# Routed experts: a third buffer for the weighed outputs, single inner buffers, and a gather issued ahead of the scatter

## The chip, the cores and the metric

The kernel runs on one core of a Trainium2 chip. The metric is the device time of one execution in microseconds (us); lower is better.

## The reference, cut to what matters

The model is x + 0.5·FFN, then x + attention, then x + 0.5·FFN again, on 4 x 1024 tokens of width 512 in float32. The two FFN halves have the same weights and hold the change. Each sends a token to 6 of 32 experts, with at most 192 tokens (slots) per expert:

```python
g = einsum('ech,eih->eci', xb, w_gate)      # xb: the tokens of expert e, gathered
u = einsum('ech,eih->eci', xb, w_up)
inter = silu(g) * u
yb = einsum('eci,ehi->ech', inter, w_down)
y = yb[eid, pos] * w_slot[:, None]          # weighed by the router
routed = y.reshape(-1, K, Hd).sum(axis=1)   # six weighed rows are added per token
```

A shared expert is added for every token; in the kernel a stage before this one computes it.

## The kernel before, in words

The program is: front, routed experts, attention, front, routed experts. `front` (n=0 and n=1) normalises the tokens, computes the router and the shared expert, stores the normalised rows in the HBM table `htab`, and makes `slots`, the row numbers of each expert's two halves of 96 tokens. The change lies in `routed_experts` alone, which runs once per FFN half, over e = 0 to 31. For one expert:

- **gather(e)** (L901, GpSimd, software queue q0): two indirect DMAs fetch 96 rows of 544 floats each from `htab` into `e_xg`. There are GATHERED = 5 such pairs of buffers, and five gathers are issued before the loop.
- **turn(e)**: TensorE transposes the rows (8 transposes, L1052), ScalarE and VectorE split them into a high and a low part (L930, L995).
- **Weights**: SyncE loads three thirds of 512 KB (L876, hardware queue q1) into one of three `e_raw` buffers; ScalarE makes the high part (L925), VectorE the low one (L989). Before the load of expert e+3, SyncE waits until scatter e-3 has landed (`added`, only for e of 3 and more) and until VectorE has split the expert e, third by third.
- **gate_up(e)**: 32 matmuls (L1063, L1064). ScalarE and VectorE add the parts, take the SiLU (L942), the product (L1009, `inter`) and split it into `in_hi` (L947) and `in_lo` (L1014).
- **down(e)**: 12 matmuls into two PSUM banks (L89 to L91).
- **weigh(e)** (L954, ScalarE): two activations write the weighed rows to `y`, which has two pairs of buffers (e % 2). So weigh(e) waits until scatter e-2 has landed. It also reads its scale from `e_xg`, so gather(e+5), which refills that buffer, may be issued only after it.
- **scatter(e)** (L909, GpSimd, q0): two indirect DMAs add 96 rows each to the result in HBM. It waits for weigh(e) and for the landing of scatter(e-1), since two experts may add to one token.

Each engine runs its own list of these steps in a written-out order. In iteration e TensorE does turn(e+1), gate_up(e), down(e-1). ScalarE does turn(e+1), two thirds of split(e+1), SiLU(e), weigh(e-1), split_inner(e), the last third of split(e+1). VectorE follows the same order. GpSimd does scatter(e), then gather(e+5) if there is one. In the first FFN half ten pieces of the attention weights are loaded and split as well. SyncE, ScalarE, VectorE and TensorE meet GpSimd only through semaphores. The stage ends when scatter(31) has landed, and the next stage begins behind it. After gather(31), which follows scatter(26), GpSimd has only scatters to issue.

Of the kernel before, what the change touches and what calls it, by code (L numbers as in the profile page):

```python
# [7 lines left out]
F32 = mybir.dt.float32  # L8
F32R = mybir.dt.float32r
# [3 lines left out]
ALU = mybir.AluOpType  # L13
ACT = mybir.ActivationFunctionType
AX = mybir.AxisListType

P = 128
B, SEQ, D = 4, 1024, 512
# [6 lines left out]
HALF = CAP // 2  # L25
# [59 lines left out]
def split_products(pe, out, hi_lo_weights, hi_lo_moving, first, last):  # L85

    wh, wl = hi_lo_weights
    mh, ml = hi_lo_moving
    pe.matmul(out, wh, mh, start=first, stop=False)  # L89
    pe.matmul(out, wh, ml, start=False, stop=False)  # L90
    return pe.matmul(out, wl, mh, start=False, stop=last)  # L91
# [731 lines left out]
def routed_experts(nc, a, k, n, htab, acc, slots, raw, xs, w_loaded, y_stored):  # L823

    with ExitStack() as ctx:
        sb = lambda name, shape, dt: ctx.enter_context(nc.sbuf_tensor(f"{name}{n}", shape, dt))
        pb = lambda name: ctx.enter_context(nc.psum_tensor(f"{name}{n}", [P, 512], F32))
        sem = lambda name: own_semaphore(nc, k, f"{name}{n}")
        TC = 2 * CAP
# [4 lines left out]
        xt = [sb(f"e_xt{u}_", [P, KB, 2, CAP], F32R) for u in range(2)]  # L834
        gate_low, up_low = sb("e_gate_low", [P, FB, CAP], F32), sb("e_up_low", [P, FB, CAP], F32)
        gate_sum, up_sum = sb("e_gate_sum", [P, FB, CAP], F32), sb("e_up_sum", [P, FB, CAP], F32)
        silu = [sb(f"e_silu{u}_", [P, TC], F32) for u in range(2)]
        inter = [sb(f"e_inter{u}_", [P, TC], F32) for u in range(2)]
        in_hi = [sb(f"e_in_hi{u}_", [P, TC], F32R) for u in range(2)]
        in_lo = [sb(f"e_in_lo{u}_", [P, TC], F32R) for u in range(2)]  # L840
        y = [[sb(f"e_y{u}{q}_", [HALF, D], F32) for q in range(2)] for u in range(2)]
        ps_t = [pb(f"e_ps_t{i}_") for i in range(2)]
        ps_gate = ctx.enter_context(nc.psum_tensor(f"e_ps_gate{n}", [P, FB * 512], F32))
        ps_up = ctx.enter_context(nc.psum_tensor(f"e_ps_up{n}", [P, FB * 512], F32))
        ps_down = [pb(f"e_ps_down{q}_") for q in range(2)]
        gathered = [sem(f"e_gathered{r}_") for r in range(GATHERED)]
        added = sem("e_added")
# [6 lines left out]
        ihi_ready, ilo_ready = sem("e_ihi_ready"), sem("e_ilo_ready")  # L854
        d_ready, y_ready = sem("e_d_ready"), sem("e_y_ready")
# [15 lines left out]
        with nc.Block(no_gpsimd_drain=True) as block:  # L871
# [24 lines left out]
            @block.gpsimd  # L896
            def _(pool):
                def gather(e):
                    for q in range(2):
                        row = bass.IndirectOffsetOnAxis(ap=slots[:, 2 * e + q:2 * e + q + 1], axis=0)  # L900
                        pool.indirect_dma_start(xg[e % GATHERED][q][:, :], None, htab, row).then_inc(gathered[e % GATHERED], 16)  # L901

                def scatter(e):
                    pool.wait_ge(y_ready, 2 * e + 2)
                    if e:
                        pool.wait_ge(added, 32 * e)
                    for q in range(2):
                        row = bass.IndirectOffsetOnAxis(ap=slots[:, 2 * e + q:2 * e + q + 1], axis=0)
                        pool.indirect_dma_start(acc, row, y[e % 2][q][:, :], None, compute_op=ALU.add).then_inc(added, 16)  # L909

                for e in range(GATHERED):
                    gather(e)
                for u in range(XS):
                    pool.wait_ge(y_stored[u], 16 * ((NT - 1 - u) // XS + 1))
                for e in range(E):
                    scatter(e)
                    if e + GATHERED < E:
                        gather(e + GATHERED)
                pool.wait_ge(added, 32 * E)

            @block.scalar
            def _(act):
                def split(e, c):
                    act.wait_ge(w_loaded[e % 3][c], 16 * (e // 3) + 16)
                    act.activation(third(w_hi[e % 2], c), third(raw[e % 3], c), ACT.Copy).then_inc(hi_ready, 1)  # L925

                def turn(e):
                    for c in range(2):
                        act.wait_ge(t_ready, 2 * e + c + 1)
                        act.activation(part(xt[e % 2], c, 0), turned(c), ACT.Copy).then_inc(t_hi, 1)  # L930

                def unload_gate(e):
                    act.wait_ge(gate_ready, e + 1)
                    act.activation(gate_low[:, :, :], low(ps_gate), ACT.Copy).then_inc(gate_low_ready, 1)

                def unload_up(e):
                    act.wait_ge(up_ready, e + 1)
                    act.activation(up_low[:, :, :], low(ps_up), ACT.Copy).then_inc(up_low_ready, 1)

                def gate(e):  # L940
                    act.wait_ge(gate_sum_ready, e + 1)
                    act.activation(silu[e % 2][:, :], gate_sum[:, :, :].rearrange("p b s -> p (b s)"),  # L942
                                   ACT.Silu).then_inc(silu_ready, 1)

                def split_inner(e):
                    act.wait_ge(mul_ready, e + 1)
                    act.activation(in_hi[e % 2][:, :], inter[e % 2][:, :], ACT.Copy).then_inc(ihi_ready, 1)  # L947

                def weigh(e):
                    if e >= 2:  # L950
                        act.wait_ge(added, 32 * (e - 1))
                    for q in range(2):
                        act.wait_ge(d_ready, 2 * e + q + 1)
                        act.activation(y[e % 2][q][:, :], ps_down[q][0:HALF, :], ACT.Copy,  # L954
                                       scale=xg[e % GATHERED][q][:, D + e:D + e + 1]).then_inc(y_ready, 1)

                def split_chunk(c):
                    hi, lo, from_ = attention_chunks[c]
                    act.wait_ge(att_loaded[c % XS], 16 * (c // XS) + 16)
                    act.activation(hi, xs[c % XS][:, :], ACT.Copy).then_inc(att_hi, 1)  # L960

                split(0, 0)
                split(0, 1)
                turn(0)
                split(0, 2)
                for e in range(E):
                    ahead = e + 1 < E
                    if ahead:
                        turn(e + 1)
                        split(e + 1, 0)  # L970
                    unload_gate(e)
                    if ahead:
                        split(e + 1, 1)
                    gate(e)
                    unload_up(e)
                    if e:
                        weigh(e - 1)
                    split_inner(e)
                    if ahead:
                        split(e + 1, 2)  # L980
                    if 0 <= e - 1 < len(attention_chunks):
                        split_chunk(e - 1)
                weigh(E - 1)

            @block.vector
            def _(dve):
# [19 lines left out]

                def gate(e):
                    dve.wait_ge(silu_ready, e + 1)
                    dve.tensor_tensor(inter[e % 2][:, :], silu[e % 2][:, :], up_sum[:, :, :].rearrange("p b s -> p (b s)"),  # L1009
                                      ALU.mult).then_inc(mul_ready, 1)  # L1010

                def split_inner(e):
                    dve.wait_ge(ihi_ready, e + 1)
                    dve.tensor_tensor(in_lo[e % 2][:, :], inter[e % 2][:, :], in_hi[e % 2][:, :].bitcast(F32),  # L1014
                                      ALU.subtract).then_inc(ilo_ready, 1)

                def split_chunk(c):
# [25 lines left out]
            def _(pe):  # L1043
# [34 lines left out]
                def down(e):  # L1078
                    w = [t[e % 2][:, WGU:].rearrange("p (k c) -> p k c", k=FB) for t in (w_hi, w_lo)]
                    pe.wait_ge(lo_ready, 3 * e + 3)  # L1080
                    pe.wait_ge(ilo_ready, e + 1)
                    for q in range(2):
                        if e:
                            pe.wait_ge(y_ready, 2 * e + q - 1)
                        for b in range(FB):
                            s = slice(b * CAP + q * HALF, b * CAP + (q + 1) * HALF)
                            got = split_products(pe, ps_down[q][0:HALF, :], (in_hi[e % 2][:, s], in_lo[e % 2][:, s]),
                                                 (w[0][:, b, :], w[1][:, b, :]), b == 0, b == FB - 1)
                        got.then_inc(d_ready, 1)

                turn(0)
                for e in range(E):
                    if e + 1 < E:
                        turn(e + 1)
                    gate_up(e)
                    if e:
                        down(e - 1)
                down(E - 1)


# [609 lines left out]
```

## Time and profile before

| what | value |
|---|---|
| median of 3 runs | 1670.54 us (1665.2 to 1672.09) |
| the profiled execution | 1662.59 us, span 1660.8 us |
| PE busy | 1476.0 us (89%) |
| VectorE, ScalarE, GpSimd busy | 1103.8, 1028.3, 754.6 us |
| 64 scatter DMAs of the first half, of the second | 96.4 us, 95.7 us on GpSimd |
| first and last scatter issue, first half | 247.58 and 527.30 us |
| first and last scatter issue, second half | 1381.37 and 1656.13 us |

All positions are in us from the start of the span. A row of the timeline gives start, duration, engine, line, operation and, in brackets, the idle time before it and what ended that. "DMA out<-e_y,slots" is the scatter in the second FFN half, "DMA x_after_ffn<-e_y,slots" that in the first.

### The profile page before, as it was taken

Reading aid. Unit: us, or ns where it says so; the run is one execution under the profiler, and the core shown is the slowest. Engines: PE = TensorE matmul, PEld = TensorE weight load, DVE = VectorE, ACT = ScalarE, POOL = GpSimd, SP = SyncE. Lnnn points to the kernel's source line nnn. Section 1 sums busy time; section 2 is a strip of 40 time slices with the busy share of each in tenths; the row PEclk is TensorE's granted clock in tenths of the full one; section 3 lists DMA queues with packets and bytes.
Section 4 is the critical chain, followed back from the end, with each engine's and each line's share of the span. In section 5 each row is a group of like instructions: output and inputs, shape, how many; then the busy total and the mean of one; then the engine's idle time right before and its main releaser. Section 6 shows DMA issues by size and latency. Waiting matters only on the chain. (4 is left out here: it accounts for less than half of the span.)

```text
span 1660.8 us, 23985 instructions
## 1 busy us (share of the span) xinstructions
PE 1476.0 (89%) x8434; PEld 1226.3 (74%) x8436; DVE 1103.8 (66%) x2094; ACT 1028.3 (62%) x2046; POOL 754.6 (45%) x655
## 2 busy tenths in 40 slices
PE   5999969989894889999999999895999869998896
PEld 4877768877773678887887887774887758877775
DVE  5659848867672466766766765664649858776774
ACT  5861448777773476666666666654762528776774
POOL 0123225655554666565556655420113224665554
PEclk9999979999997799999999999997999979999998
DMA  7736388989895101111111111006654467998895
GB/s 275 246 126 207 99 260 249 266 257 265 258 264 87 52 26 46 39 58 52 39 39 64 39 39 39 30 35 232 204 178 153 144 205 231 259 270 250 263 257 104
DMA packets 113207, 257.61 MB, mean 155 GB/s; under 512 B 21216, under 2 KB 22176, under 8 KB 112832
## 3 DMA queue, kind: packets, MB, share of 16 engines
q1 hardware_dynamic: 90560, 204.16, 37.3%
q0 software_dynamic: 22528, 51.92, 13.8%
q8 instruction: 68, 1.11, 0.3%
q14 instruction: 51, 0.42, 0.1%
HBM read 187.27 MB, written 68.76 MB: 154 GB/s over the span
## 5 line engine op out<-in xcount | busy, mean ns | idle before, releaser
L989 DVE TENSOR_TENSOR e_w_lo<-e_raw,e_w_hi 128x1024 fp32r<-128x1024 f32 x192 | 233.9, 1219 | 31.2 <-ACT e_w_hi L925 29.6
L925 ACT ACTIVATE e_w_hi<-e_raw 128x1024 fp32r<-128x1024 f32 x192 | 202.3, 1054 | 20.8 <-PEq L273 20.8
L1490 POOL TENSOR_SCALAR t_prob<-t_prob,t_inv 128x128 f32<-128x128 f32 (+7 forms) x128 | 111.5, 871 | 221.3 <-DVE t_inv L1395 221.3
L901 POOL DMA_INDIRECT e_xg<-htab,slots x128 | 145.7, 1138 | 58.0 <-issue 38.4
L1063 PE MATMUL e_ps_gate<-e_xt,e_w_hi 128*128 128x384 f32 x512 | 159.3, 375 | 0.0
L909 POOL DMA_INDIRECT x_after_ffn<-e_y,slots x64 | 96.4, 1506 | 121.8 <-ACT e_y L954 83.9
L1063 PE MATMUL e_ps_up<-e_xt,e_w_hi 128*128 128x384 f32 x512 | 151.0, 360 | 0.0
L909 POOL DMA_INDIRECT out<-e_y,slots x64 | 95.7, 1495 | 120.9 <-ACT e_y L954 83.6
L357 POOL TENSOR_SCALAR d_inter<-d_inter 128x512 f32<-128x512 f32 x32 | 26.2, 818 | 266.9 <-DVE d_inter L521 266.8
L1290 ACT ACTIVATE t_prob<-a_wide,t_neg_max,a_q_scale 128x128 f32<-128x128 f32 (+7 forms) x128 | 106.5, 832 | 53.8 <-DVE t_neg_max L1389 53.5
L954 ACT ACTIVATE e_y<-e_ps_down,e_xg 96x512 f32<-96x512 f32 x128 | 83.1, 679 | 90.5 <-DMA out<-e_y,slots 34.2
L1064 PE MATMUL e_ps_gate<-e_xt,e_w_lo 128*128 128x192 f32 x512 | 130.5, 255 | 0.0
L1064 PE MATMUL e_ps_up<-e_xt,e_w_lo 128*128 128x192 f32 x512 | 128.4, 251 | 0.0
L1297 ACT ACTIVATE t_pt<-a_bank 128x512 fp32r<-128x512 f32 x144 | 84.0, 596 | 68.4 <-PE a_bank L1566 68.1
L1400 DVE TENSOR_TENSOR t_pt<-a_bank,t_pt 128x512 fp32r<-128x512 f32 x144 | 96.2, 684 | 41.6 <-ACT t_pt L1297 41.0
L1052 PE MATMUL e_ps_t<-ident,e_xg 96*128 96x96 f32 x512 | 58.1, 259 | 69.2 <-DMA e_xg<-htab,slots 69.2
L1052 PEld LDWEIGHTS e_ps_t<-ident,e_xg 96*128 96x128 f32 x512 | 48.0, 146 | 93.5 <-DMA e_xg<-htab,slots 91.4
L1014 DVE TENSOR_TENSOR e_in_lo<-e_inter,e_in_hi 128x384 fp32r<-128x384 f32 x64 | 35.8, 559 | 111.8 <-ACT e_in_hi L947 108.8
L89 PE MATMUL e_ps_down<-e_w_hi,e_in_hi 128*96 128x512 f32 x256 | 101.4, 396 | 3.6 <-issue 3.6
L91 PE MATMUL e_ps_down<-e_w_hi,e_in_lo 128*96 128x512 f32 x256 | 101.8, 398 | 0.0
L90 PE MATMUL e_ps_down<-e_w_lo,e_in_hi 128*96 128x512 f32 x256 | 100.9, 394 | 0.0
L1064 PEld LDWEIGHTS e_ps_gate<-e_xt,e_w_lo 128*128 128x128 f32 x512 | 100.8, 197 | 0.1
(218 smaller groups left out, 4613.5 us busy)
## 6 DMA issues: line engine op xcount, KB each, us to landing
e_raw<-in_w_experts SPq DMA_DIRECT2D x192, 512.0 KB
htab<-d_h SPq DMA_DIRECT2D x16, 1024.0 KB, 5.2
d_x<-in_x SPq DMA_DIRECT2D x16, 512.0 KB, 6.9
d_xs<-in_x SPq DMA_DIRECT2D x32, 256.0 KB, 3.5
x_after_ffn<-d_xs SPq DMA_DIRECT2D x32, 256.0 KB, 3.2
q_x<-x_after_ffn SPq DMA_DIRECT2D x32, 256.0 KB, 3.0
t_res<-x_after_ffn SPq DMA_DIRECT2D x32, 256.0 KB, 2.6
x_after_attention<-t_res SPq DMA_DIRECT2D x32, 256.0 KB, 2.0
```

Of the source, the lines that this page charges most:

```text
L89: pe.matmul(out, wh, mh, start=first, stop=False)
L90: pe.matmul(out, wh, ml, start=False, stop=False)
L91: return pe.matmul(out, wl, mh, start=False, stop=last)
L901: pool.indirect_dma_start(xg[e % GATHERED][q][:, :], None, htab, row).then_inc(gathered[e % GATHERED], 16)
L909: pool.indirect_dma_start(acc, row, y[e % 2][q][:, :], None, compute_op=ALU.add).then_inc(added, 16)
L925: act.activation(third(w_hi[e % 2], c), third(raw[e % 3], c), ACT.Copy).then_inc(hi_ready, 1)
L989: dve.tensor_tensor(third(w_lo[e % 2], c), third(raw[e % 3], c), third(w_hi[e % 2], c).bitcast(F32), ALU.subtract).then_inc(lo_ready, 1)
L1052: got = pe.transpose(ps_t[c][:, at:at + HALF], xg[e % GATHERED][q][:, (2 * c + b) * P:(2 * c + b + 1) * P], k.ident[0:HALF, 0:HALF])
L1063: pe.matmul(out, w[0][:, c, cols], xt[e % 2][:, c, :, :], start=c == 0, stop=False)
L1064: got = pe.matmul(out[:, 0:CAP], w[1][:, c, cols], xt[e % 2][:, c, 0, :], start=False, stop=c == KB - 1)
L1290: act.activation(prob[:, u, 0:width(i)], ps_s[i % 2][:, 0:width(i)], ACT.Exp, scale=q_scale[:, i // H % QSLOTS, i % H:i % H + 1], bias=neg ...
L1490: pool.tensor_scalar(prob[:, u, 0:width(i)], prob[:, u, 0:width(i)], inv[:, u:u + 1], 1.0, ALU.mult, ALU.mult).then_inc(p_ready, 1)
```

## The change

`silu`, `inter`, `in_hi` and `in_lo` get one buffer each in place of two. `y` gets a third pair of buffers, so weigh(e) waits for the landing of scatter e-3. GpSimd's loop waits for weigh(e) first, then issues gather(e+5), and then waits for the landing of scatter(e-1) and issues scatter(e).

```diff
-        silu = [sb(f"e_silu{u}_", [P, TC], F32) for u in range(2)]
-        inter = [sb(f"e_inter{u}_", [P, TC], F32) for u in range(2)]
-        in_hi = [sb(f"e_in_hi{u}_", [P, TC], F32R) for u in range(2)]
-        in_lo = [sb(f"e_in_lo{u}_", [P, TC], F32R) for u in range(2)]
-        y = [[sb(f"e_y{u}{q}_", [HALF, D], F32) for q in range(2)] for u in range(2)]
+        silu = sb("e_silu", [P, TC], F32)
+        inter = sb("e_inter", [P, TC], F32)
+        in_hi = sb("e_in_hi", [P, TC], F32R)
+        in_lo = sb("e_in_lo", [P, TC], F32R)
+        y = [[sb(f"e_y{r}{q}_", [HALF, D], F32) for q in range(2)] for r in range(3)]
...
                 def scatter(e):
-                    pool.wait_ge(y_ready, 2 * e + 2)
                     if e:
                         pool.wait_ge(added, 32 * e)
...
-                        pool.indirect_dma_start(acc, row, y[e % 2][q][:, :], None, compute_op=ALU.add).then_inc(added, 16)
+                        pool.indirect_dma_start(acc, row, y[e % 3][q][:, :], None, compute_op=ALU.add).then_inc(added, 16)
...
                 for e in range(E):
-                    scatter(e)
+                    pool.wait_ge(y_ready, 2 * e + 2)
                     if e + GATHERED < E:
                         gather(e + GATHERED)
+                    scatter(e)
...
                 def weigh(e):
-                    if e >= 2:
-                        act.wait_ge(added, 32 * (e - 1))
+                    if e >= 3:
+                        act.wait_ge(added, 32 * (e - 2))
```

The remaining lines replace `[e % 2]` of the four inner buffers by the single one, and `y[e % 2]` by `y[e % 3]`.

## Rows read from the trace of the kernel before

**Rows 1.** The page: its head, and its chain that ended last, by line.
```profile
span 1660.8 us, 23985 instructions
...
DMA out<-e_y,slots 11%; POOL out L909 3%; ACT e_y L954 1%; DMA e_xg<-htab,slots 1%; POOL e_xg L901 0%; PE e_ps_gate L1063 0%; PE e_ps_up L1063 0%; PE e_ps_t L1052 0%; DVE e_w_lo L989 0%; PE e_ps_gate L1064 0%; PE e_ps_up L1064 0%; ACT e_w_hi L925 0%; PE e_ps_down L91 0%; PE e_ps_down L89 0%; DVE e_xt L995 0%
```

**Rows 2.** Windows: stretch, length, busy PE, PEld, DVE, ACT, POOL, PEclk, DMA, GB/s.
```profile
1390.50:1444.40 53.90, 53.10 (x340) 46.49 (x338) 44.05 (x62) 43.28 (x73) 34.69 (x24) 1.00 0.91 266
1444.40:1527.30 82.90, 73.96 (x468) 63.53 (x468) 58.34 (x81) 59.86 (x100) 46.44 (x37) 1.00 0.88 260
```

**Rows 3.** The chain that ended last, in order of time, 1501 to 1518.
```profile
1501.26 6.73 DMA out<-e_y,slots
...
1508.01 0.69 ACT e_y L954
...
1508.79 1.47 POOL out L909
...
1510.56 6.14 DMA out<-e_y,slots
...
1517.50 1.46 POOL out L909
```

**Rows 4.** Waits, 1450 to 1600: total, times, longest (us).
```profile
POOL out L909 <- ACT e_y L954: 52.8, 17, 4.0
...
ACT e_y L954 <- DMA out<-e_y,slots: 27.6, 16, 2.7
PEld e_ps_t L1052 <- DMA e_xg<-htab,slots: 22.8, 16, 2.1
```

**Rows 5.** Waits of the queue on SyncE, 1376 to 1445, and 1445 to 1620.
```profile
SPq L876 <- DMA out<-e_y,slots: 45.8, 7, 8.4
...
SPq L876 <- DMA out<-e_y,slots: 147.0, 19, 8.6
```

**Rows 6.** DMA queues (packets, MB, share), 1509.8 to 1512.8, and 1514.2 to 1517.2.
```profile
q1 hardware_dynamic: 315, 1.16, 97.3%
...
q0 software_dynamic: 315, 0.75, 101.2%
```

**Rows 7.** Timeline of GpSimd, start of the second stage, then of the first.
```profile
1381.37 1.83 POOL L909 DMA_INDIRECT out<-e_y,slots  x1 [18.88 <-ACT e_y L954]
1383.51 1.44 POOL L909 DMA_INDIRECT out<-e_y,slots  x1 [0.30 <-issue]
1385.25 1.07 POOL L901 DMA_INDIRECT e_xg<-htab,slots  x1 [0.30 <-issue]
1386.62 1.29 POOL L901 DMA_INDIRECT e_xg<-htab,slots  x1 [0.30 <-issue]
1389.88 2.44 POOL L909 DMA_INDIRECT out<-e_y,slots  x1 [1.96 <-DMA out<-e_y,slots]
...
257.75 1.46 POOL L909 DMA_INDIRECT x_after_ffn<-e_y,slots  x1 [2.96 <-DMA x_after_ffn<-e_y,slots]
```

**Rows 8.** Timeline of ScalarE: weigh(0), (1), (2) second half, (8); weigh(1) of the first stage.
```profile
1379.24 1.25 ACT L954 ACTIVATE e_y<-e_ps_down,e_xg 96x512 f32<-96x512 f32 x2
1386.79 1.36 ACT L954 ACTIVATE e_y<-e_ps_down,e_xg 96x512 f32<-96x512 f32 x2
1395.46 0.68 ACT L954 ACTIVATE e_y<-e_ps_down,e_xg 96x512 f32<-96x512 f32 x1 [0.45 <-PE e_ps_down L91]
1443.64 1.29 ACT L954 ACTIVATE e_y<-e_ps_down,e_xg 96x512 f32<-96x512 f32 x2 [1.44 <-DMA out<-e_y,slots]
...
253.66 1.25 ACT L954 ACTIVATE e_y<-e_ps_down,e_xg 96x512 f32<-96x512 f32 x2
```

**Rows 9.** The chain that ended last, at its end: the scatter with no other traffic.
```profile
1642.78 4.25 DMA out<-e_y,slots
1647.79 1.41 POOL out L909
```

**Rows 10.** Windows, behind the first stage (columns as in Rows 2).
```profile
528.00:536.00 8.00, 0.00 (x0) 0.00 (x0) 1.25 (x2) 1.28 (x1) 0.72 (x1) 0.50 0.62 136
```

More of the change, by code:

```diff
@@ L941, in gate @@
                     act.wait_ge(gate_sum_ready, e + 1)
-                    act.activation(silu[e % 2][:, :], gate_sum[:, :, :].rearrange("p b s -> p (b s)"),
+                    act.activation(silu[:, :], gate_sum[:, :, :].rearrange("p b s -> p (b s)"),
                                    ACT.Silu).then_inc(silu_ready, 1)
@@ L946, in split_inner @@
                     act.wait_ge(mul_ready, e + 1)
-                    act.activation(in_hi[e % 2][:, :], inter[e % 2][:, :], ACT.Copy).then_inc(ihi_ready, 1)
+                    act.activation(in_hi[:, :], inter[:, :], ACT.Copy).then_inc(ihi_ready, 1)
                 def weigh(e):
-                    if e >= 2:
-                        act.wait_ge(added, 32 * (e - 1))
+                    if e >= 3:
+                        act.wait_ge(added, 32 * (e - 2))
                     for q in range(2):
                         act.wait_ge(d_ready, 2 * e + q + 1)
-                        act.activation(y[e % 2][q][:, :], ps_down[q][0:HALF, :], ACT.Copy,
+                        act.activation(y[e % 3][q][:, :], ps_down[q][0:HALF, :], ACT.Copy,
                                        scale=xg[e % GATHERED][q][:, D + e:D + e + 1]).then_inc(y_ready, 1)
@@ L1008, in gate @@
                     dve.wait_ge(silu_ready, e + 1)
-                    dve.tensor_tensor(inter[e % 2][:, :], silu[e % 2][:, :], up_sum[:, :, :].rearrange("p b s -> p (b s)"),
+                    dve.tensor_tensor(inter[:, :], silu[:, :], up_sum[:, :, :].rearrange("p b s -> p (b s)"),
                                       ALU.mult).then_inc(mul_ready, 1)
@@ L1013, in split_inner @@
                     dve.wait_ge(ihi_ready, e + 1)
-                    dve.tensor_tensor(in_lo[e % 2][:, :], inter[e % 2][:, :], in_hi[e % 2][:, :].bitcast(F32),
+                    dve.tensor_tensor(in_lo[:, :], inter[:, :], in_hi[:, :].bitcast(F32),
                                       ALU.subtract).then_inc(ilo_ready, 1)
@@ L1086, in down @@
                             s = slice(b * CAP + q * HALF, b * CAP + (q + 1) * HALF)
-                            got = split_products(pe, ps_down[q][0:HALF, :], (in_hi[e % 2][:, s], in_lo[e % 2][:, s]),
+                            got = split_products(pe, ps_down[q][0:HALF, :], (in_hi[:, s], in_lo[:, s]),
                                                  (w[0][:, b, :], w[1][:, b, :]), b == 0, b == FB - 1)
```

## The prediction

> **What bounds the kernel now.** I read the chain that ended last on the page first [rows 1]. What it names for the last stage is one thing: the scatter's DMA, 11% of the span, with its issue on GpSimd, 3%. In the table of stretches [rows 2] the reader is to see two regimes in one stage. From 1390.5 to 1444.4 TensorE is busy 53.10 of 53.90 us; an expert is 52 matmuls and transposes (8 + 32 + 12), so 340 of them are 6.5 experts at 8.2 us each. From 1444.4 on it is busy 89%, and 468 are 9.0 experts in 82.9 us, 9.2 us each. The clock is full in both. So TensorE could run at 8.2 and is held to 9.2.
>
> The chain in order of time says by what [rows 3]. The second half of scatter(13) is issued at 1501.26 and lands 6.73 us later, at 1507.99; weigh(15) starts at 1508.01; scatter(14) is issued at 1508.79. The profile puts ScalarE between them, but weigh(15) fills the buffer for scatter(15), and scatter(14) waits for landing(13) alone: it starts 0.80 us after it, as scatter(31) does where ScalarE has long been done (landing at 1642.78 + 4.25 = 1647.03 for scatter(30), issue at 1647.79, 0.76 later [rows 9]). The loop is therefore: first issue 1.47, gap 0.30, second issue to landing 6.14, wake 0.80 = 8.71 us, and 9.1 on average. It is strictly serial over 32 experts and no buffer is in it. The waits of ScalarE for the scatter (16 times, 27.6 us) and of TensorE for the gather (16 times, 22.8 us) [rows 4] are the other engines held to that loop: one through the `y` buffer, one because the gather is issued behind the scatter.
>
> What fills 6 to 7 us of landing, when the last scatters need 4.25 [rows 9]? SyncE's loads wait for the same landing, 7 times to 1445 and in all 19 experts of 1445 to 1620, for 147.0 us [rows 5], so 1.5 MB of weights start at each landing. The queues show it [rows 6]: in 1509.8 to 1512.8 the hardware queue holds 97.3% of the engines and q0 moves nothing, though scatter(14) and a gather have been issued; in 1514.2 to 1517.2 q0 has them. Landing, weights, then scatter, is one cycle.
>
> **The change, part by part.**
>
> *Single inner buffers.* ScalarE writes `in_hi`(e) behind weigh(e-1), which has waited for down(e-1), the reader of the old one; VectorE's writes come behind its own reads and ScalarE's. The written order covers them: 0. If it did not, a copy would be late on an engine that gains 0.9 us per expert on the scatters.
>
> *Third `y` buffer.* Removed: weigh(e)'s wait for landing(e-2); in its place is landing(e-3). ScalarE and TensorE may run one expert further ahead. They gain about 9.1 - 8.2 = 0.9 us per expert, so the wait that now begins at weigh(8) [rows 8] begins some ten experts later and then comes back at the same size. Next late is the gather, then the weights: load(e+3) is released by landing(e-3), so a third needed about 3 us behind a landing would just arrive. None of it reaches the scatter loop, which has its `y` ready either way. On the path: 0. If that cover were gone, ScalarE's 27.6 us / 16 = 1.7 us per expert would be the price.
>
> *Gather ahead, in the steady stretch.* Scatter(e-1)'s second issue ends about 4 us after landing(e-2). weigh(e) is done by 1.3 us after landing(e-2) even with two buffers [rows 3], earlier with three. So GpSimd finds `y_ready` set and issues gather(e+5) at once behind scatter(e-1), in the very place where gather(e+4) is now. Its order of instructions and q0's order of packets are the same, with the gather's number one higher. Both run under the landing. SyncE's loads are tied to the landings as before. Cost 0 per expert.
>
> *Gather ahead, at the start.* Here there is no cover. GpSimd is free and waits for weigh(0), done at 1380.49 [rows 8]; scatter(0) follows at 1381.37. Now gather(5) is put between: 1.07 + 0.30 + 1.29 + 0.30 = 2.96 us as they stand behind the scatter [rows 7]. Scatter(0)'s two issues move by that. Its landing moves by less or by more: second issue 1383.51, landing 1389.88 - 0.80 = 1389.08, so 5.57, of which 4.25 is needed without traffic. A weight third that shares this time would be over: at best the landing moves by 2.96 - 1.32 = 1.6; with the gather's rows ahead in q0 (a half of the 0.75 MB that took 3 us [rows 6], 1.5 us) at worst by 4.5. I take 2.5, near the issues' own time, the nearest row.
>
> Expert 1: weigh(1) is done at 1388.15, GpSimd starts gather(6) at about 1389.0 and ends it at 1391.9; landing(0) is now at 1391.6, scatter(1) could go at 1392.4. Hidden on GpSimd, but its rows are ahead in q0 just when the weights burst starts: between 0 and 1.5 us, I take 0.5. Expert 2: weigh(2) is done at 1396.14, scatter(1)'s issues end near 1396, so the gather starts a microsecond later than now: 0. From expert 3 on the lead is enough.
>
> The first FFN half: weigh(1) is done at 254.91 and scatter(1) starts at 257.75 [rows 7, 8], a wider cover; scatter(0) is followed by the same pair. Again 2.5.
>
> *The end.* gather(31) moves from behind scatter(26) to behind scatter(25). Its rows come behind the scatter's: between 0 and -1.5 us, I take 0. TensorE ends a period earlier, but it is already at the 1.2 GHz level (0.50) before attention starts [rows 10], so its clock there is unchanged: 0.
>
> Sum: 2 x 2.5 + 0.5 = 5.5, with bounds 2 x 1.6 - 2 x 1.5 = 0 and 2 x (4.5 + 1.5) = 12. I take +5. The profiled execution is 1662.59 (span 1660.8), 8 us under the median of 1670.54; on that median's scale the forecast is 1675.5, its own range 1669 to 1683. About 0.5% (8 us) is what a measurement of this kernel can tell from no change.
>
> **The rivals.**
>
> *A, slower: the gather delays the scatters beyond the start.* Place: GpSimd, between `y_ready`(e) and scatter(e). It decides where weigh(e) ends later than about 2 us before landing(e-1), since the two gather issues take 2.5 to 3. In the stages' first experts the lead is 0.9 us at expert 1 (1388.15 against 1389.08) and grows by 0.9 each. If three experts per stage pay 2.96 and 1.5 us of rows in q0: 2 x 3 x 4.46 = +27; with issues alone +18. For: it is certain for e = 0. Against: every later `y_ready` is ahead. Middle +20: 1690.5.
>
> *B, slower: VectorE at full pace lengthens the issues.* In the stretch where VectorE does not wait, a scatter issue took 2.44 us (1389.88) against 1.47 [rows 7, 3]; it lies in the serial loop. The change lengthens that stretch by some ten experts per stage: 2 x 10 x 0.97 = +19 at most, with the 5: 1695. Against: the stretch before 1444 has the same 9.1 us per scatter, since the scatter's rows wait for the weights anyway. The Trainium skill ("SBUF — State Buffer", "Who interferes with whom") says that a VectorE instruction with two SBUF inputs contends with a GpSimd one that reads SBUF; the long issue above agrees.
>
> *C, faster: landings get shorter.* Two neighbours take 6.73 and 6.14 us [rows 3], and I do not know why. If TensorE's and ScalarE's lead shifts the traffic so that all take the short one, 0.6 us for half of 50 steady experts is 15 us, and 30 if for all: with the 5 added, about 1660, down to 1645. Against: loads and scatters are both tied to the landing.
>
> *D: no change at all,* the start hidden by shorter contention: 1670.5. It lies in the forecast's own range.
>
> The Trainium skill ("DMA: Bandwidth & Descriptors", "Queues, rings and completion order") says that an engine takes turns between queues packet by packet; by that the scatter would share with the weights, where here q0 moved nothing for 3 us. By the page a gather ahead in q0 would cost about twice its own 1.5 us, by the row 1.5.
>
> **How the numbers follow.** Forecast with D 0.67 (nine tenths of it within 0.5%, the rest slower), A 0.10, B 0.05, C 0.15, other 0.03, shared. Faster: C's larger part and a little of the rest, 0.14. Slower: A, B and the forecast's upper tail, 0.20. Same: 0.66. The range 1660 to 1689 holds the forecast, D, half of A and half of C.
>
> **What the profile would show.** Right: GpSimd issues two gathers, then scatter(0), some 3 us later after weigh(0) than now; from expert 3 on the sequence is scatter, scatter, gather, gather; the mean step between scatters stays at 9.1; ScalarE's wait for the scatter starts near expert 18; 3 to 5 us more between weigh(0) and the last landing of each stage. Wrong: a step between scatters that differs from 9.1 by over 0.2 us (6 us per stage), gathers between a landing and a scatter behind expert 3, or weights loads no longer released by the landing.

## The result and the profile after

The changed kernel has a median of 1673.22 us (1668.40 to 1675.36, 12 runs) against 1666.97 us of the kernel before (1663.64 to 1672.09, 12 runs): ratio 1.0033, 95% interval 1.0018 to 1.0048, so 5.5 us slower. (Where a cost in us is given for a kernel, it is this ratio less 1, times the median of the kernel before; the two medians themselves are 6.25 us apart.) Forecast were +5 and "within 0.5%". The absolute forecast of 1675.5 stood on a median of three runs, 1670.54, which twelve runs put at 1666.97. The profiled execution took 1668.4 us, its span is 1666.5.

The page of the changed kernel, its head and the chain by line (as [rows 1]):

```profile
span 1666.5 us, 23931 instructions
...
DMA out<-e_y,slots 12%; POOL out L908 3%; POOL e_xg L901 1%; DMA e_xg<-htab,slots 0%; ACT e_y L954 0%; PE e_ps_gate L1063 0%; DVE e_w_lo L989 0%; PE e_ps_up L1063 0%; PE e_ps_t L1052 0%; PE e_ps_gate L1064 0%; ACT e_w_hi L925 0%; DVE e_xt L995 0%; ACT e_up_low L938 0%; PE e_ps_up L1064 0%; DVE e_inter L1009 0%
```

The scatter is still what the last stage is made of. GpSimd's timeline at the start of the second stage, as [rows 7]:

```profile
1382.02 0.92 POOL L901 DMA_INDIRECT e_xg<-htab,slots  x1 [18.98 <-ACT e_y L954]
1383.25 1.72 POOL L901 DMA_INDIRECT e_xg<-htab,slots  x1 [0.31 <-issue]
1385.27 2.36 POOL L908 DMA_INDIRECT out<-e_y,slots  x1 [0.30 <-issue]
1387.93 1.45 POOL L908 DMA_INDIRECT out<-e_y,slots  x1 [0.30 <-issue]
1389.68 1.25 POOL L901 DMA_INDIRECT e_xg<-htab,slots  x1 [0.30 <-issue]
1391.24 1.31 POOL L901 DMA_INDIRECT e_xg<-htab,slots  x1 [0.30 <-issue]
1392.85 2.27 POOL L908 DMA_INDIRECT out<-e_y,slots  x1 [0.30 <-issue]
...
1403.27 1.46 POOL L908 DMA_INDIRECT out<-e_y,slots  x1 [3.03 <-DMA out<-e_y,slots]
```

gather(5) stands ahead of scatter(0), which starts 5.29 us behind the start of weigh(0) (1379.98) and not 2.13. gather(6) already stands directly behind scatter(0)'s second issue, in the place that gather(5) had; scatter(1) follows it at once, and from scatter(2) on GpSimd waits for the landing again. In the first stage the same rows are:

```profile
248.96 1.49 POOL L908 DMA_INDIRECT x_after_ffn<-e_y,slots  x1 [0.30 <-issue]
250.76 1.45 POOL L908 DMA_INDIRECT x_after_ffn<-e_y,slots  x1 [0.30 <-issue]
...
255.87 1.49 POOL L908 DMA_INDIRECT x_after_ffn<-e_y,slots  x1 [0.30 <-DMA x_after_ffn<-e_y,slots]
```

Here scatter(1) follows scatter(0) after 6.91 us, where it took 10.17 before (247.58 to 257.75): the delayed scatter(0) landed at most 4.3 us behind its second issue, as the last scatters do that meet no weights. From weigh(0) to scatter(2) the first stage lost 0.9 us and the second 3.3 (against the second profile of before, told below, 1.0 and 2.4).

The waits of 1450 to 1600 (as [rows 4]) and, below the dots, SyncE's from 1445 to 1620 (as [rows 5]): total, times, longest.

```profile
POOL out L908 <- DMA out<-e_y,slots: 40.2, 17, 3.7
...
ACT e_y L954 <- DMA out<-e_y,slots: 22.3, 15, 2.4
PEld e_ps_t L1052 <- DMA e_xg<-htab,slots: 19.7, 15, 1.8
...
ACT e_w_hi L925 <- DMA e_raw<-in_w_experts: 5.7, 15, 0.6
...
SPq L876 <- DMA out<-e_y,slots: 147.1, 19, 9.3
```

As forecast, the stalls came back at nearly their size (ScalarE's 22.3 us against 27.6, TensorE's 19.7 against 22.8), the loads are released by the landings as before (147.1 against 147.0 us), and a new small wait for the weights, 5.7 us in 15 times, stands where a third of weights "would just arrive". The windows (columns as in [rows 2]):

```profile
1391.20:1449.00 57.80, 57.80 (x379) 51.81 (x378) 47.45 (x67) 47.94 (x81) 35.76 (x26) 1.00 0.89 256
1449.00:1532.00 83.00, 76.37 (x483) 65.61 (x481) 62.01 (x86) 61.54 (x103) 52.84 (x37) 1.00 0.89 260
```

TensorE's lead goes on longer, and ScalarE first waits for a landing at weigh(11):

```profile
1467.31 1.48 ACT L954 ACTIVATE e_y<-e_ps_down,e_xg 96x512 f32<-96x512 f32 x2 [0.42 <-DMA out<-e_y,slots]
```

The mean step between scatters 3 and 26 is 9.22 us in the first stage and 9.18 in the second, against 9.18 and 9.15 before. That difference is inside what one kernel shows from execution to execution, as the run named before_again tells below. So one trace shows a start that costs something, and cannot show whether the steady stretch costs a tenth of a microsecond per expert. The medians had to decide that.

### The profile page after: what moved, and what is told of

Its sections match the earlier page's. It is cut to its first block and busy times, and to the rows that moved or that the text cites. A ratio compares the mean times of both kernels' runs of the same rounds, so it can differ in the third digit from the quotient of the medians.

```text
span 1666.5 us, 23931 instructions
## 1 busy us (share of the span) xinstructions
PE 1472.3 (88%) x8434; PEld 1224.6 (73%) x8436; DVE 1104.7 (66%) x2094; ACT 1028.9 (62%) x2046; POOL 771.3 (46%) x655
## 5 line engine op out<-in xcount | busy, mean ns | idle before, releaser
L989 DVE TENSOR_TENSOR e_w_lo<-e_raw,e_w_hi 128x1024 fp32r<-128x1024 f32 x192 | 234.2, 1221 | 34.0 <-ACT e_w_hi L925 29.8
L901 POOL DMA_INDIRECT e_xg<-htab,slots x128 | 158.7, 1240 | 96.8 <-ACT e_y L954 40.3
L908 POOL DMA_INDIRECT out<-e_y,slots x64 | 100.1, 1565 | 95.0 <-DMA out<-e_y,slots 71.0
L908 POOL DMA_INDIRECT x_after_ffn<-e_y,slots x64 | 97.4, 1522 | 98.2 <-DMA x_after_ffn<-e_y,slots 74.0
```

The source lines that it names most:

```text
L908: pool.indirect_dma_start(acc, row, y[e % 3][q][:, :], None, compute_op=ALU.add).then_inc(added, 16)
L989: dve.tensor_tensor(third(w_lo[e % 2], c), third(raw[e % 3], c), third(w_hi[e % 2], c).bitcast(F32), ALU.subtract).then_inc(lo_ready, 1)
```

## The experiments

**Theory T** (the prediction's): the loop of scatters is the bound; only the gather ahead of scatter(0) costs. **Rival R**: the other engines' greater lead lengthens the landings.

**The two parts alone.** third_buffer_only restores the old order on top of the changed kernel:

```diff
                     pool.wait_ge(y_ready, 2 * e + 2)
+                    scatter(e)
                     if e + GATHERED < E:
                         gather(e + GATHERED)
-                    scatter(e)
```

> Third y buffer and single inner buffers, with the gather behind the scatter as before. Theory T (the loop of scatters is the bound, and only the gather put ahead of scatter(0) costs): no change against the kernel before, ratio 0.999 to 1.001; scatter(0) again 0.9 us behind the end of weigh(0), the step from scatter(26) to scatter(27) again about 9.0. Rival R (the greater lead of the other engines shifts the traffic and lengthens the landings): slower, 1.002 to 1.004, with the loss spread over the experts.

Measured: 1671.42 us, 1.0028 (1.0018 to 1.0038). T is wrong here and R has the size: the third buffer alone, which I had put at 0, costs 4.7 us. R's premise, the greater lead, is looked at below. gather_ahead_only puts the new order into the kernel before, with two `y` buffers:

> The new order on GpSimd with two y buffers and the old inner buffers. T: the whole loss of the change, ratio 1.002 to 1.005, in the first expert of each stage (scatter(0) 3 to 4 us behind weigh(0)). R: no change, since the lead is that of the kernel before.

Measured: 1671.52 us, 1.0028 (1.0017 to 1.0039). T has the size of this part, and scatter(0) starts 5.3 us behind the start of weigh(0) as it says. But from weigh(0) to scatter(2) the two stages lose 3.3 us together (2.5 against the second profile of before), so T's "in the first expert" leaves 1.4 to 2.2 us without a place. The parts cost 4.7 us each and together 5.5, so they do not add up: either one costs 0.28% in the kernel before and about 0.05% on top of the other (1.0033 against 1.0028, inside the intervals).

first_gather_behind takes the changed kernel and moves gather(5) alone back:

```diff
-                    if e + GATHERED < E:
+                    if e and e + GATHERED < E:
                         gather(e + GATHERED)
                     scatter(e)
+                    if e == 0:
+                        gather(GATHERED)
```

> The changed kernel, but gather(5) alone goes back behind scatter(0); gather(6) and the later ones stay ahead. T: most of the loss is gone, ratio 1.000 to 1.002 (what is left is gather(6) ahead of scatter(1)). If the loss comes from the later experts or from the end of the stage, where scatter(27) started 10.1 us behind scatter(26) in the changed kernel: still 1.002 to 1.004.

Measured: 1672.73 us, 1.0022 (1.0010 to 1.0034). This is T's miss (1.000 to 1.002) and inside the other forecast. 0.0011 or 1.8 us less than the changed kernel, within both intervals. The start may hold a part of the loss, not most of it. What is left has the size of the third buffer's own cost, but that it is that cost is not shown.

**Is it the freed wait, or the layout?** third_buffer_no_lead keeps three buffers and the layout of third_buffer_only but the old wait:

```diff
-                    if e >= 3:
-                        act.wait_ge(added, 32 * (e - 2))
+                    if e >= 2:
+                        act.wait_ge(added, 32 * (e - 1))
```

> As third_buffer_only (three y buffers, single inner ones, gather behind the scatter), but weigh(e) waits for landing(e-2) as in the kernel before, so that ScalarE and TensorE cannot run further ahead. third_buffer_only measured 1.0028. If the lead makes that loss (theory L): 0.999 to 1.001, mean step between scatters 3 to 26 back at 9.1 to 9.2, and the second scatter issue back at 1.44 us from 1.62. If the other places of the buffers in SBUF make it (rival P): 1.002 to 1.004, step 9.3.

Measured: 1667.95 us, 0.9999 (0.9988 to 1.0010). The intervals of third_buffer_only (1.0018 to 1.0038) and of this kernel (0.9988 to 1.0010) do not meet. It is the wait that weigh(e) no longer has, and neither the layout nor the single inner buffers. The forecast of the step, back at 9.1 to 9.2, missed: it is 9.27 and 9.30 us here and 9.30 and 9.35 in third_buffer_only, and one trace does not tell these apart.

The name is misleading in one thing: third_buffer_only has no greater lead to lose. From expert 8 to 25 weigh(e) ends on average 7.7 and 8.1 us before landing(e-1) in its two stages, against 7.8 and 7.8 in the kernel before. The gather, issued behind the scatter, still holds TensorE (23.8 us in 15 waits from 1450 to 1600, against 22.8 in 16), and through it ScalarE. Only where the gather is ahead as well, in the changed kernel, does the lead grow, to 16.1 us. Weigh(14), second half, and scatter(14) in third_buffer_only; then weigh(15) and scatter(15) in the changed kernel:

```profile
1502.47 0.68 ACT L954 ACTIVATE e_y<-e_ps_down,e_xg 96x512 f32<-96x512 f32 x1 [0.65 <-PE e_ps_down L91]
1512.40 1.47 POOL L908 DMA_INDIRECT out<-e_y,slots  x1 [1.82 <-DMA out<-e_y,slots]
```

```profile
1504.66 1.26 ACT L954 ACTIVATE e_y<-e_ps_down,e_xg 96x512 f32<-96x512 f32 x2 [1.26 <-DMA out<-e_y,slots]
1523.23 1.47 POOL L908 DMA_INDIRECT out<-e_y,slots  x1 [2.65 <-DMA out<-e_y,slots]
```

So a greater lead, R's mechanism, does not explain the 4.7 us of third_buffer_only. What the pages do show are GpSimd's issues. For each kernel: all gathers, then the scatters of the first stage. Before_again, third_buffer_no_lead, third_buffer_only, and the changed kernel; last, the gathers of gather_ahead_only:

```profile
L901 POOL DMA_INDIRECT e_xg<-htab,slots x128 | 146.4, 1144 | 58.0 <-issue 38.4
L909 POOL DMA_INDIRECT x_after_ffn<-e_y,slots x64 | 97.0, 1515 | 119.5 <-ACT e_y L954 77.7
```

```profile
L901 POOL DMA_INDIRECT e_xg<-htab,slots x128 | 149.3, 1167 | 58.0 <-issue 38.4
L908 POOL DMA_INDIRECT x_after_ffn<-e_y,slots x64 | 99.5, 1554 | 117.2 <-ACT e_y L954 62.7
```

```profile
L901 POOL DMA_INDIRECT e_xg<-htab,slots x128 | 158.0, 1234 | 58.0 <-issue 38.4
L908 POOL DMA_INDIRECT x_after_ffn<-e_y,slots x64 | 101.0, 1578 | 111.5 <-ACT e_y L954 62.8
```

```profile
L901 POOL DMA_INDIRECT e_xg<-htab,slots x128 | 158.7, 1240 | 96.8 <-ACT e_y L954 40.3
L908 POOL DMA_INDIRECT x_after_ffn<-e_y,slots x64 | 97.4, 1522 | 98.2 <-DMA x_after_ffn<-e_y,slots 74.0
```

```profile
L901 POOL DMA_INDIRECT e_xg<-htab,slots x128 | 160.8, 1256 | 95.1 <-ACT e_y L954 38.3
```

GpSimd's issues become longer: the 128 gathers go from 146 and 149 to 158 us. The scatters' second issues, experts 8 to 25, take 1.58 to 1.66 us on average in third_buffer_only and 1.56 to 1.59 in the changed kernel, against 1.44 to 1.51 in third_buffer_no_lead and the two profiles of before. That is rival B's sign. But it does not come from a lead: gather_ahead_only, with two `y` buffers, has it too (160.8 us, and 1.56 to 1.57). Nor is VectorE busier under the issues: it works in 96 to 97% of the gathers' time before and in 91% in third_buffer_only and third_buffer_no_lead alike. What has changed is that a gather beside its split of the weights takes longer (L989: 1.32 and 1.33 us in the two profiles of before, 1.37 in third_buffer_no_lead, 1.41 in third_buffer_only, 1.59 in gather_ahead_only); why is not known. So every kernel of this group that is 0.2 to 0.3% slower has longer issues, which would also fit that the two parts do not add up. Whether they are the price is the next question.

before_again, the kernel before once more:

> The kernel before once more, for a second profile: how much the mean step between scatters (9.1 in the first), the durations of the issues and the totals of the stages (308.4 and 304.1 us from the first gather to the last scatter issue) scatter between executions of one kernel. If the differences between the variants are of the kernel, the second scatter issue is again at 1.44 us and the totals stay within 2 us; if they are of the execution, they move by as much as between the variants, 5 us.

Measured: 1669.03 us. The second scatter issue takes 1.47 and 1.44 us on average (experts 8 to 25), as in the first profile (1.44 both times); as far as two executions tell, it belongs to the kernel. From the first gather to the last scatter issue the stages took 306.0 and 309.8 us against 308.4 and 304.1: up to 5.7 us apart. So totals and mean steps (9.33 against 9.14 from scatter 8 to 26 of the second stage) do not separate kernels that differ by 0.3%.

**What stands in the loop?** gather_behind_landing makes each gather wait for landing(e-1):

```diff
                     if e + GATHERED < E:
+                        if e:
+                            pool.wait_ge(added, 32 * e)
                         gather(e + GATHERED)
```

> The changed kernel, but gather(e+5) waits for landing(e-1) like the scatter, so that both its issues stand openly in the loop between landing and scatter in 26 experts of each stage. If the issue time is in the loop in full, 2.5 us x 52 = 130 us slower (ratio 1.078), with the gather's rows in q0 ahead up to 3.5 x 52 = 180 (1.11). If the weights burst behind each landing covers the issues, since the scatter's rows wait for it anyway, only the rows ahead in q0 count: 1.2 to 1.5 us x 52 = 62 to 78 us (1.037 to 1.047).

Measured: 1740.88 us, 1.0435 (1.0420 to 1.0450), 72.5 us: the covered case. Beside the changed kernel, which it differs from by this edit alone, it is 67 us or 1.3 per expert. GpSimd's timeline of this kernel:

```profile
1504.18 0.96 POOL L901 DMA_INDIRECT e_xg<-htab,slots  x1 [3.68 <-DMA out<-e_y,slots]
1505.45 1.69 POOL L901 DMA_INDIRECT e_xg<-htab,slots  x1 [0.30 <-issue]
1507.44 1.51 POOL L908 DMA_INDIRECT out<-e_y,slots  x1 [0.30 <-issue]
1509.26 1.43 POOL L908 DMA_INDIRECT out<-e_y,slots  x1 [0.30 <-issue]
1514.28 1.55 POOL L901 DMA_INDIRECT e_xg<-htab,slots  x1 [3.58 <-DMA out<-e_y,slots]
```

The gathers add 3.26 us ahead of the scatter, but from its second issue to the landing (0.8 before 1514.28) it is 4.2 us now and not 6.1 to 6.7 [rows 3]. The burst of weights has passed by the time the scatter's rows come. Some 2 us of this delay behind the landing are covered.

issue_delay puts two memsets, each with a drain, at the same place in third_buffer_no_lead:

```diff
                         pool.wait_ge(added, 32 * e)
+                        pool.memset(pad[:, :], 0.0)
+                        pool.drain()
+                        pool.memset(pad[:, :], 0.0)
+                        pool.drain()
```

> third_buffer_no_lead (0.9999 of the kernel before) with two memsets of 128x480 on GpSimd between the landing of scatter(e-1) and the issue of scatter(e), some 1.0 to 1.4 us with their drains in 31 experts of each stage. If the issue time stands in the loop in full: 62 to 87 us slower, ratio 1.037 to 1.052; then the longer issues of the variants with a lead (2 to 5 us per stage) explain their 0.3 per cent. If the weights burst behind the landing covers it: at most the last 5 experts of each stage, which have no load, pay, 10 to 14 us, ratio 1.006 to 1.008; then longer issues are not the cause.

Measured: 1821.91 us, 1.0928 (1.0897 to 1.0960), outside both. The dose was not what I meant it to be:

```profile
1536.17 0.51 POOL L907 MEMSET e_pad<- 128x480 f32 x1
1539.85 0.50 POOL L909 MEMSET e_pad<- 128x480 f32 x1 [3.17 <-issue]
1541.18 1.47 POOL L913 DMA_INDIRECT out<-e_y,slots  x1 [0.83 <-issue]
1542.95 1.67 POOL L913 DMA_INDIRECT out<-e_y,slots  x1 [0.30 <-issue]
1544.92 0.97 POOL L902 DMA_INDIRECT e_xg<-htab,slots  x1 [0.30 <-issue]
1546.19 1.76 POOL L902 DMA_INDIRECT e_xg<-htab,slots  x1 [0.30 <-issue]
1547.95 0.52 POOL L907 MEMSET e_pad<- 128x480 f32 x1
```

The first drain, behind the gathers, holds GpSimd for 3.17 us, and GpSimd itself is the bound: it has no wait for a landing left in a step of 11.8 us. ScalarE's weigh, released at 1535.86, shows landing to issue as 5.3 us and not 0.8. As a test of a small dose it failed. It leaves rival B undecided: 4.5 us more before the issue lengthened the step from 9.3 to 11.7, so here too about 2 us were covered, which speaks against a price for issues that are 0.1 to 0.2 us longer; but no small dose was measured, and both doses lie ahead of the first issue, not in the second.

**Is it the weights that make the landing long?** small_loads:

```diff
-                    sp.dma_start(third(raw[e % 3], c), third(a["w_experts"][e, :, :], c)).then_inc(w_loaded[e % 3][c], 16)
+                    size = THIRD if e < 6 else THIRD // 4
+                    sp.dma_start(third(raw[e % 3], c)[:, 0:size], third(a["w_experts"][e, :, :], c)[:, 0:size]).then_inc(w_loaded[e % 3][c], 16)
```

> The changed kernel with the weights of expert 6 and later loaded to a quarter only (the rest of each third keeps what an earlier expert left there). If weights traffic fills the landing, it falls to the 4.2 to 4.3 us of the last scatters, the loop would take 1.77 + 4.3 + 0.8 = 6.9 us, TensorE becomes the bound and the step is 8.0 to 8.2: 0.9 to 1.1 x 22 x 2 = 40 to 48 us faster, ratio 0.971 to 0.976. If the landing is long for another reason (the accumulation in HBM, the gather behind it): step 9.0 and no change.

This kernel leaves out three quarters of the weights from expert 6 on. Measured: 1606.1 us, 0.9634 (0.9618 to 0.9649). The window from 1400 to 1500 (columns as in [rows 2]):

```profile
1400.00:1500.00 100.00, 100.00 (x649) 89.14 (x648) 81.81 (x115) 81.77 (x138) 82.27 (x51) 1.00 0.77 153
```

TensorE never stops, 52 instructions take 8.0 us, and scatters follow each other in 7.99 us. The bound has moved as forecast; it gained 61 us and not 40 to 48: the steps fell by 1.2 us, which over 23 experts of two stages is 55, and the first steps shrank too. loads_ungated keeps the bytes and removes the tie:

```diff
-                    if e >= 3:
-                        sp.wait_ge(added, 32 * (e - 2))
```

> The changed kernel without SyncE's wait for the landing of scatter e-3; the loads follow VectorE's splits alone. If the burst of weights at each landing is what makes the scatter's landing 6 to 7 us (the cycle of the prediction): the loads spread out, the step between scatters falls from 9.1 towards TensorE's 8.2, at most 0.9 x 26 x 2 = 47 us faster, ratio 0.97 to 0.99. If the DMA engines' total work is the bound, however it is spread (busy 0.90): no change or up to 1 per cent slower, step 9.1 to 9.3.

Measured: 1648.48 us, 0.9889 (0.9874 to 0.9903). The same edit without the change, before_ungated:

> The kernel before, with SyncE's loads freed from the landing of scatter e-3, nothing else. The changed kernel with that edit measured 0.9889. If the change's third buffer and order are of use once the loads no longer come in a burst at the landing: this one is slower than that, 0.992 to 0.997. If the gain is the gate's alone and the change costs its 0.3 per cent here too: 0.984 to 0.987.

Measured: 1667.35 us, 0.9998 (0.9984 to 1.0013), slower than either case: here the freed loads gain nothing, and the change is worth 1.1%. third_ungated:

> The same edit on third_buffer_only (three y buffers, gather behind the scatter). Beside before_ungated it tells what the lead does without the burst: if the lead's loss came from its meeting with the burst, this is equal to before_ungated or faster by up to 0.5 per cent; if not, slower by 0.3 per cent.

Measured: 1666.36 us, 0.9984 (0.9969 to 1.0000): beside before_ungated no clear difference, and not the 0.3% of third_buffer_only. By the forecast's own terms the third buffer's loss then came from its meeting with the burst of loads behind each landing. Its second scatter issues are long here too (1.56 and 1.61 us) and cost nothing that shows, which speaks against rival B. What is left to make use of the freed loads is the order on GpSimd, and the last kernel, ahead_ungated, has just that with two `y` buffers:

> gather_ahead_only (two y buffers, the gather ahead of the scatter) with the loads freed from the landing. Against the kernel before, the freed loads gave 0.9998 without the change, 0.9984 with the third buffer alone, 0.9889 with the whole change. If the order on GpSimd is what makes use of the freed loads: 0.987 to 0.992. If order and third buffer are needed together: 0.996 to 1.001.

Measured: 1626.7 us, 0.9750 (0.9732 to 0.9769), beyond the forecast of the first case and the fastest kernel of this study that computes the whole reference. Windows of 1400 to 1600 (columns as in [rows 2]) of before, before_ungated, loads_ungated and ahead_ungated:

```profile
1400.00:1600.00 200.00, 183.27 (x1161) 157.83 (x1160) 146.01 (x203) 147.95 (x247) 115.75 (x89) 1.00 0.90 263
```

```profile
1400.00:1600.00 200.00, 184.12 (x1145) 162.33 (x1144) 145.74 (x201) 147.06 (x245) 123.45 (x88) 0.97 0.97 264
```

```profile
1400.00:1600.00 200.00, 191.39 (x1209) 170.42 (x1208) 153.22 (x212) 153.37 (x256) 134.68 (x94) 0.97 1.01 280
```

```profile
1400.00:1600.00 200.00, 195.91 (x1263) 173.94 (x1263) 157.19 (x220) 158.95 (x267) 135.41 (x94) 1.00 1.01 275
```

Instructions in brackets tell the pace: 1161, 1145, 1209 and 1263 in 200 us, or 9.0, 9.1, 8.6 and 8.2 us per expert. With the loads freed TensorE still waits for gathers, whether they stand behind the scatter (before_ungated) or ahead of it with three `y` buffers (loads_ungated), and the waits are few and long. The waits of the one and then of the other, 1480 to 1600:

```profile
PEld e_ps_t L1050 <- DMA e_xg<-htab,slots: 11.5, 6, 4.1
```

```profile
PEld e_ps_t L1050 <- DMA e_xg<-htab,slots: 10.3, 4, 4.8
```

In ahead_ungated that wait is absent from 1480 to 1600, and TensorE's clock is full. Against it loads_ungated has the third `y` buffer, and the single inner ones, and is 1.4% slower (0.9889 against 0.9750). Here the slower kernel does have the longer lead: weigh(e) ends 11.7 and 10.3 us before landing(e-1), against 6.6 and 6.4 (experts 8 to 25). Which of the two buffer changes costs the 1.4% was not tried.

## Why the prediction was right, and which step of it was not

- *The bound.* Right, and shown. Less weights traffic brings the step to TensorE's 8.0 us; a scatter whose issue comes behind the burst lands in 4.2 us.
- *Single inner buffers, 0.* Right where it was tried: third_buffer_no_lead has them and measures 0.9999. Together with the long lead of the changed kernel they were not tried apart.
- *Third `y` buffer, 0.* **Wrong**, taken alone: it costs 0.28%, 4.7 us, and with the old wait at weigh(e) nothing; on top of the gather ahead it adds 0.05%, which is no clear difference. The step that failed is "None of it reaches the scatter loop". I had reasoned about waits, and no wait does reach it. Nor does ScalarE run "one expert further ahead" by the third buffer alone: its lead stays at 8 us until the gather goes ahead too. What the freed wait does reach is GpSimd's issues (gathers 146 to 158 us), the sign of rival B, which I had given 0.05. That these longer issues are the price is not shown: the delay experiments speak for some 2 us of cover, and third_ungated has long issues and no loss. How the step grows by 0.09 us (an estimate, 4.7 us over 52 experts) stays open; third_ungated speaks for the burst of loads having a part in it.
- *Gather ahead in the steady stretch, 0.* Right as far as the order goes: from scatter(2) on the trace has scatter, scatter, gather, gather, wait. Its place matters: 1.3 us per expert where it is put behind the landing.
- *Gather ahead at the start, 2.5 + 0.5 and 2.5.* The issue moved by 3.2 us (2.96 forecast). Of that the stages kept 0.9 and 3.3 us at scatter(2), 4.2 together against the 5.5 of the sum (3.4 against the second profile of before). gather_ahead_only costs 4.7 us, of which its start shows 2.5 to 3.3; moving gather(5) back gave 1.8 us less with an interval that includes none.
- *The end, 0; the clock, 0.* The clock was at its 1.2 GHz level in both before attention (0.50 from 528 to 536). The step from scatter(26) to (27), where no gather is behind the scatter now, was 10.42 and 10.12 us, against 9.27, 8.88, 9.07 and 9.24 in the two profiles of before. It was 10.93 and 9.75 in first_gather_behind, 9.28 and 9.56 in gather_ahead_only. I had allowed 0 to -1.5 and it looks like +1 per stage; the cause was not tried.
- *ScalarE's wait begins near expert 18.* It begins at weigh(11), in the first stage at weigh(12). TensorE's pace is 8.0 us and not 8.2, in the kernel before as well (there weigh(3) to weigh(7) of the second stage follow each other in 7.99 us), and the scatters started 3 to 4 us later, so the lead filled sooner.

The sum, +5 against +5.5, is near the measurement partly by luck. The stages' starts carry 3.4 to 4.2 us of it, and I had looked for no other cost; that the third buffer's 4.7 us nearly vanish on top of the gather's 4.7 was no part of the reasoning.

## What to carry to other kernels

When a chain of DMAs is the bound, an added buffer for a faster engine gains nothing and can cost: here 0.28% alone, though no wait of the chain had changed. Look also whether the buffer gives any lead at all, or whether another wait, here TensorE's for the gather, holds the engine at the same place. Ask first what makes a link of the chain long; here a wait tied every load to the very landing that also releases the next scatter, and freeing it paid only once the gather was issued ahead. Try the parts of a change alone and with each other's bound removed: the new order on GpSimd costs 0.3% in the kernel as it was and gains 2.5% beside freed loads, where the third buffer, with the single inner ones, gives 1.4% of it back.

## What the runs showed that I had not expected

- Behind a landing ScalarE starts within 0.02 us and GpSimd's indirect DMA after 0.8. In issue_delay's last steps the memset starts 0.1 us after the landing, and the indirect DMA 0.79 us after the second memset, so most of the 0.8 lies ahead of the DMA instruction and is not the wake. The chain of that kernel, in order of time (L908 and L910 are the drains; the chain names them for the time of the memsets, which start at 1806.11 and 1806.90):

```profile
1801.72 4.28 DMA out<-e_y,slots
1806.10 0.51 POOLq L908
...
1806.89 0.51 POOLq L910
1807.40 0.79 issue
1808.19 1.43 POOL out L913
```

- A drain on GpSimd behind two gathers held it for 3.17 us; behind nothing but a memset it took 0.29.
- With the loads in a burst q0 moved nothing for 3 us [rows 6]; with the loads spread (ahead_ungated) both queues move packets in the same microsecond (from 1510 to 1511 q1 takes 74.5% and q0 38.4%), and the engines' busy share goes from 0.90 to 1.01.
